# Key-major score pieces of a cross-attention kernel dealt over slots 1 to 7 of a unit by the matmul work of each slot

## What is computed

```
q = x @ Wq.T + bq;  k = ctx @ Wk.T + bk;  v = ctx @ Wv.T + bv        (split into 16 heads of 32)
att = softmax(q k^T / sqrt(32))                                      (per head, 224 x 750)
out = x + (att @ v) @ Wo.T + bo
out = (out - mean) / sqrt(var + 1e-5) * gamma + beta                 (over the 512)
```

## Time and profile before

| | |
|---|---|
| median of 3 runs | 680.19 us (678.84 to 680.62) |
| the profiled execution, its time | 678.81 us |
| the profiled execution, its span | 676.4 us |
| mean granted clock of PE | 0.988 |
| busy PE / DVE / ACT / POOL | 645.8 / 476.1 / 331.9 / 455.4 us |

### The profile page before, as it was taken

How to read it: one execution, slowest core, us unless ns; L and a number is a source line. 1 busy time by engine, 2 the same in 40 slices (tenths; PEclk the granted TensorE clock), 3 DMA queues, 4 the chain that set the end, 5 groups by cost and what they waited for, 6 DMA issues and landing times.

```text
span 676.4 us, 15102 instructions
## 1 busy us (share of the span) xinstructions
PE 645.8 (95%) x5433; PEld 448.0 (66%) x5433; DVE 476.1 (70%) x680; ACT 331.9 (49%) x657; POOL 455.4 (67%) x458
## 2 busy tenths in 40 slices
PE   6999999999999999999999999999999999997893
PEld 5756666766767666776767667776677767664451
DVE  4657667787767786777767787677867877664875
ACT  4514545455555455554455545555455545543470
POOL 9302765866967588576857679575867759675962
PEclk9999999999999999999999999999999999998798
DMA  9383323232232223332233322322233201330010
GB/s 289 113 210 89 82 75 75 53 95 51 74 98 70 65 74 86 85 71 88 56 82 84 88 74 56 95 70 67 83 81 90 51 1 41 93 80 23 1 56 28
DMA packets 39514, 53.08 MB, mean 78 GB/s; under 512 B 13388, under 2 KB 25688, under 8 KB 39448
## 3 DMA queue, kind: packets, MB, share of 16 engines
q1 hardware_dynamic: 39448, 52.16, 28.9%
HBM read 24.52 MB, written 3.67 MB: 42 GB/s over the span
## 4 chain that ended last, share of the span: by engine, by line
PE 86%; DVE 7%; issue 3%; POOL 2%; DMA 1%; ACT 1%; SPq 0%; POOLq 0%; DVEq 0%; ACTq 0%
PE ps_task L472 38%; PE ps_scores L483 11%; PE ps_task L521 11%; PE ps_scoresT L507 10%; PE ps_task L436 6%; PE ps_scores L472 3%; PE ps_task L446 2%; DVE top L741 2%; PE ps_task L547 2%; DMA ctx_in<-in_ctx 1%; DVE y L715 1%; PE ps_scoresT L492 1%; PE ps_task L450 1%; POOL pair_sums L850 1%; DVE parts L703 1%
## 5 line engine op out<-in xcount | busy, mean ns | idle before, releaser
L741 DVE TENSOR_REDUCE top<-ps_scores 112x1 f32<-112x750 f32 x256 | 235.4, 926 | 120.7 <-PE ps_scores L483 120.3
L850 POOL TENSOR_TENSOR pair_sums<-probsT 125x672 f32<-125x672 f32 x122 | 198.8, 1629 | 174.8 <-ACT probsT L642 169.7
L642 ACT ACTIVATE probsT<-ps_scoresT 125x448 f32<-125x448 f32 x384 | 189.0, 548 | 111.2 <-PE ps_scoresT L507 107.8
L483 PE MATMUL ps_scores<-stacks 96*112 96x512 f16 (+1 forms) x512 | 125.6, 327 | 4.3 <-DVE top L741 3.0
L472 PE MATMUL ps_task<-wvT,ctxT 128*125 128x512 f16 x552 | 127.2, 380 | 0.7 <-DVE ctxT L705 0.6
L472 PE MATMUL ps_task<-ctxT,wkT 128*128 128x375 f16 x696 | 120.7, 323 | 0.1
L507 PE MATMUL ps_scoresT<-stacks 100*125 100x224 f16 x768 | 116.9, 265 | 2.3 <-ACT probsT L642 0.4
L507 PEld LDWEIGHTS ps_scoresT<-stacks 100*125 100x125 f16 x768 | 81.6, 136 | 35.2 <-ACT probsT L642 18.4
L472 PEld LDWEIGHTS ps_task<-wvT,ctxT 128*125 128x125 f16 x552 | 73.0, 136 | 38.9 <-DVE ctxT L705 0.9
L472 PEld LDWEIGHTS ps_task<-ctxT,wkT 128*128 128x128 f16 x696 | 67.6, 97 | 36.8 <-DVE v L708 0.5
L855 POOL TENSOR_TENSOR head_sums<-pair_sums 125x224 f32<-125x224 f32 x122 | 84.5, 693 | 10.4
(11 more groups left out here) (96 smaller groups left out, 599.2 us busy)
## 6 DMA issues: line engine op xcount, KB each, us to landing
stacks<-parts SPq DMA_DIRECT2D x256, 60.9 KB, 2.0
ctx_in<-in_ctx SPq DMA_DIRECT2D x16, 672.0 KB
stacks<-parts SPq DMA_DIRECT2D x128, 46.9 KB, 2.0
x_in<-in_x SPq DMA_DIRECT2D x8, 448.0 KB, 3.7
resid<-in_x SPq DMA_DIRECT2D x8, 448.0 KB, 3.8
out_y<-y SPq DMA_DIRECT2D x16, 224.0 KB, 2.3
stacks<-parts SPq DMA_DIRECT2D x128, 14.0 KB, 1.8
ctx_in<-in_ctx SPq DMA_DIRECT2D x16, 78.0 KB
```

Source lines behind the costliest of these rows:

```text
L483: last = nc.tensor.matmul(ps_scores[0:QP, s % RING, keys], stacks[0:STACK_ROWS, g, h, NK + QP * q:NK + QP * q + QP], stacks[0:STACK_ROWS, ...
L642: nc.scalar.activation(probsT[0:KP, g % 2, h, 2 * j:2 * j + 2, :].rearrange("p k q -> p (k q)"), ps_scoresT[0:KP, piece % 2, 0:2 * NQ], AC ...
L741: nc.vector.tensor_reduce(top[0:QP, g % 2, HG * q + h:HG * q + h + 1], ps_scores[0:QP, s % RING, 0:NK], AX.X, ALU.max).then_inc(top_ready, 1)
L850: nc.gpsimd.tensor_tensor(pair_sums[0:KP], probsT[0:KP, g % 2, h, 0:3, :], probsT[0:KP, g % 2, h, 3:6, :], ALU.add).then_inc(pair_sums_rea ...
```

## The change

It replaces the rule for the pieces by a table over the 32 steps, and in the visit's slot it puts the pieces behind the attends and ahead of the sums. In a unit the pieces still come in their order and are still twelve. Slot 0 has none, slot 1 has two; of the steps with transposes, 2, 6, 10, 12, 20 and 23 have one, 14 has two and 16 (a slot 0) none; steps 30 and 31 have one each; the others have two. ACT's iteration follows the same function, so its two first exps of a unit move to slot 1, ahead of the copy.

```diff
+    PIECES_IN = (0, 2, 1, 2, 2, 2, 1, 2,  0, 2, 1, 2, 1, 2, 2, 2,  0, 2, 2, 2, 1, 2, 2, 1,  0, 2, 2, 2, 2, 2, 1, 1)
...
+    assert all(sum(PIECES_IN[i:i + UNIT]) == PIECES for i in range(0, STEPS, UNIT))
...
         def pieces_of(s):
 
-            i = s % UNIT
-            return (2 * i - 4, 2 * i - 3) if i >= 2 else ()
+            of_slot = PIECES_IN[UNIT * (s // UNIT):s + 1]
+            return range(sum(of_slot[:-1]), sum(of_slot))
...
                         if s % UNIT == 0:
                             turn_maxima(u, (g - 1) % UNITS)
-                        for piece in pieces_of(s):
-                            scores_keymajor(u, (g - 1) % UNITS, piece)
+                        if s % UNIT != VISIT:
+                            for piece in pieces_of(s):
+                                scores_keymajor(u, (g - 1) % UNITS, piece)
                     if due(("attend", 0), b, s) and not (isinstance(b, int) and b == B):
                         pe.wait_ge(task_saved, before + saved_by(b, s - TASK_BANKS))
                     for k in range(KT):
                         for u, g_u in due(("attend", k), b, s):
                             attend(u, g_u, k, b if g >= 2 else b - 1, parity if g >= 2 else 1 - parity)
+                    u = unit_before(b, g, 1)
+                    if u is not None and s % UNIT == VISIT:
+                        for piece in pieces_of(s):
+                            scores_keymajor(u, (g - 1) % UNITS, piece)
                     for u, g_u in due("sum_keys", b, s):
                         sum_keys(u, g_u)
```

## The result

The changed kernel takes 685.25 us (median of 4, 685.04 to 686.95) against 679.52 us (median of 4) for the kernel before: a ratio of 1.0083, 95% interval 1.0064 to 1.0102. It is slower, by 0.8%. The forecast was 685.1 us, within 681.7 to 688.3. The profiled execution was the slowest of the four, 686.95 us around a span of 684.8.

A forecast was written before the change was run, and what follows sets the result against it. PE, busy 77.29 of a middle batch's 77.48 us, was taken as the bound. Hand-overs +7.3, stalls -2.2 and batch 7 -0.2 gave +4.9 us on the 680.19 us median: 685.1 us, range 681.7 to 688.3.

The forecast's parts named there:

- The hand-over, 0.28 us a visit: Pieces between attends and sums: one more round trip into 32-column work, 0.28 us a visit, +7.3 us over 26 visits.
- Maxima and copy cost nothing: In the visit, piece 0's wait for ACT's maxima and the later copy of the sums add nothing.
- The stalls, unit by unit: Steps with one piece: unit 0 -0.30, unit 1 -0.15 and -0.11, unit 2 +0.19, unit 3 0 us a batch.
- unit 1: Slot 11's stall goes, -0.15 us; slots 12 and 13 give -0.11, between -0.35 and +0.10; slot 14's stall stays.
- Slot 21 lost what slot 20 gave: Unit 2: the piece removed from slot 20 returns as wait for DVE's save in slot 21, +0.19 us.
- the -0.37: Sum of the stall changes per full batch, -0.37 us; -2.2 us for six batches, batch 0 left at 0.
- Batch 7, -0.2 forecast: Last batch, no next one to prepare: stalls, visit, slot 17 and slot 25 sum to -0.2 us.
- three sub-steps: Batch 7: stalls after slots 2 and 6 -0.65 us, POOL's head sum at slot 17 -0.46, slot 25 +0.66.
- the final slots at 0: Final slots of batch 7: same pieces and as many hand-overs, so 0 us.
- A (free hand-over): Rival: hand-over between last attend and piece 0 is free; -2.9 us in all, 677.3 us; chance 0.07.
- D (the copy holds PE): Rival: the visit's exps delay the copy, holding PE in slots 2 and 3; +5.2 us, 690.3 us; chance 0.04.
- B (all stalls go): Rival: dealing clears every short stall, slot 21's DVE wait too; 1.3 us a batch, 679.4 us; chance 0.08.
- C (the clock is kept in slot 18 of batch 7): Rival: slot 17's wait ends sooner, PE may keep 2.4 GHz; -1.7 us, 683.4 us; chance 0.11.

The follow-up runs named there:

- the hand-over alone: Kernel before the change, no piece moved; in the visit's slot the next step's two score matmuls stand between attends and sums: 694.95 us, ratio 1.022.
- the fastest kernel: Changed kernel with the visit's pieces ahead of the attends and the old deal (two pieces in slots 2 to 7) in units 2 and 3: 675.26 us, ratio 0.9935.

## Why the prediction was right

**The hand-over, 0.28 us a visit.** Right in size and in parts (0.12, 0.13, 0.03 forecast; 0.11, 0.14, 0.03 measured), and shown as the cause of the loss in a middle batch by four runs: absent with the pieces behind the sums or ahead of the attends, present with no piece moved, and the same for one piece as for two. Reading it from the tail of the old kernel, where the very order already stood, was what made it exact.

**Maxima and copy cost nothing.** Right for batches 5 and 6: PE has no such wait in slots 1 to 3, and with the same ACT order but the pieces ahead of the attends the loss goes. In batches 1 to 4 of the changed kernel there is a small wait that the prediction put at nothing: the first pair behind the visit in units 2 and 3 takes 0.46 to 0.68 us to the next task for 0.39, about 1 us in all. In slot 18 of batch 1 PE's weight load (PEld) waits for ACT's exps. They start 0.88 us behind the visit's pair there, and 0.45 in batch 6; why is open:

```profile
152.12 0.60 PE L509 MATMUL ps_scoresT<-stacks 100*125 100x224 f16 x4
153.00 0.98 ACT L649 ACTIVATE probsT<-ps_scoresT 125x448 f32<-125x448 f32 x2 [2.41 <-PE ps_scoresT L509]
153.60 0.19 PEld L509 LDWEIGHTS ps_scoresT<-stacks 100*125 100x125 f16 x2 [0.25 <-ACT probsT L649]
```

**The stalls, unit by unit.** Forecast for a middle batch, hand-over included: unit 2 +0.47, unit 3 +0.28, unit 0 -0.02, unit 1 +0.02, in all +0.75. Measured from attends to attends: +0.46, +0.28, -0.01, -0.07, in all +0.66. The doubtful one was unit 1: the stall of slot 13 left whole (0.19 us), where I had allowed 0.11 for slots 12 and 13, and slot 15 stayed at 0.58 us, so DVE followed PE a little further than I allowed. Slot 21 lost what slot 20 gave, as said, and the run with slot 20 refilled gives the 0.20 us back.

**Batches 0 to 6 together** lost 3.7 us by slot 17 of batch 6, where the same terms count 24 x 0.28 - 6 x 0.56 (units 0 and 1) + 5 x 0.19 (unit 2) = 4.3. The term at fault is the -0.37, which I took from the late batches; the loss per batch was below 0.75 us in five of the six intervals from slot 17 to slot 17 (0.39, 0.54, 0.58, 0.57, 0.84, 0.66). In batches 1 to 4 the parts differ from the late ones and partly cancel. Unit 0 won 0.16 to 0.17 us and unit 1 0.20 to 0.48, as the pairs of slots 3 and 11 had taken 0.68 us there and not 0.53; unit 2 lost 0.55 to 0.83 and unit 3 0.37 to 0.40, with the wait for the exps above.

**Batch 7, -0.2 forecast.** Here three sub-steps were off. Slots 3 and 7 kept 0.33 us of stall each instead of 0.2 and 0.3. POOL's second head did start 0.44 us earlier behind the value task, but the sums came no earlier: one of POOL's adds took 1.08 us instead of 0.69. It lay over a scaling of DVE's, which in the kernel before had begun 0.26 us ahead of the add (the last section has such a pair; here it is not tested):

```profile
614.30 1.08 POOL L862 TENSOR_TENSOR head_sums<-pair_sums 125x224 f32<-125x224 f32 x1
614.48 0.38 DVE L762 TENSOR_TENSOR attn<-attn_sums,recip 128x224 f32<-128x224 f32 x1
```

And from slot 25 to the last turn of the maxima the changed kernel lost 0.48 us, not 0.66. The scores of slot 26 came 0.96 us later, as a pair, a round trip and more time in the attends (4.64 us for 4.34) stood ahead of them, but DVE was not the bound all the way: its scaling took 0.38 us for 0.67, and the old turn had come 0.24 us behind the maxima, released by an exp. PE's wait in slot 17, in the answer on PE's waits:

```profile
PE ps_task L549 <- POOL head_sums L865: 3.0, 1, 3.0
```

It shrank from 3.52 to 3.01 only because a pair of pieces now stands in it. At the last turn of the maxima the changed kernel was 4.9 us late (652.94 against 648.03): the forecast's sum, with a shortfall of 0.6 in the middle and an excess of 0.7 from slot 17 of batch 6 on that cancelled, which is luck.

**The last 3.5 us of the profiled execution** are the step that failed: the prediction has the final slots at 0, as they hold the same pieces and as many hand-overs. From the last turn to the end the changed kernel took 31.8 us, the one before 28.4. The windows over the same kind of work, of the changed kernel and of the one before:

```profile
655.90:662.00 6.10, 6.10 (x49) 2.71 (x48) 2.59 (x2) 2.50 (x5) 3.14 (x3) 0.50 0.01 3
```

```profile
649.90:655.80 5.90, 5.87 (x87) 3.16 (x86) 3.31 (x4) 4.41 (x9) 4.28 (x5) 1.00 0.06 17
```

Here PE ran at half its clock, 1.2 GHz, and made 49 matmul records in 6.10 us where 87 took 5.90. Just ahead stood its waits for DVE's maxima (1.33 us) and for an exp (0.44). In the kernel before the turn had waited 0.76 us. The windows of 14 us from the last turn, of the changed kernel, the one before, the hand-over alone and the fastest kernel, in this order:

```profile
652.94:666.94 14.00, 13.46 (x146) 6.77 (x146) 7.50 (x6) 7.48 (x16) 5.80 (x6) 0.76 0.10 32
648.03:662.03 14.00, 13.90 (x186) 7.67 (x187) 8.51 (x9) 8.52 (x17) 6.01 (x6) 1.00 0.11 35
664.66:678.66 14.00, 13.91 (x187) 7.67 (x188) 8.57 (x9) 8.50 (x17) 5.48 (x5) 1.00 0.11 35
641.87:655.87 14.00, 12.98 (x166) 6.73 (x170) 7.36 (x7) 8.08 (x16) 5.98 (x6) 0.88 0.11 35
```

The granted clock of this window is 0.76 or 0.88 in all nine profiled executions with a table of pieces, which take 30.9 to 32.2 us from the last turn to the end, and 1.00 in the two without (28.4 us each). So in the profiles the lower clock comes with the table, which also deals the pieces of the final slots anew. There is one profile of each kernel, and no run tests which of the waits ahead brings it. It doesn't stand in the medians in full: the other three executions of the changed kernel have spans of 682.5 to 683.5 us.

**The total.** The sum to the last turn was right, the end was not, and the median came out at 685.25 against 685.1 with some luck. The forecast put its 4.9 us on a median of 680.19 us, while the profiled execution, whose rows it used, was 1.4 us faster. Between the two profiled executions the change costs 8.1 us (686.95 against 678.81), between the medians of four 5.7.

**The rivals.** A (free hand-over) and D (the copy holds PE) are ruled out for the middle batch by the rows of the visit. B (all stalls go) fails at slot 21, and also at slot 15, where the pair still takes 0.58 us and the value task still starts 0.06 us behind DVE's save. C (the clock is kept in slot 18 of batch 7) did not happen: the output projection took 4.44 us there, 4.09 before.

## What to carry to other kernels

On an engine that is busy for more than 99% of a batch, read distances between starts, not waits: this loss had no wait to its name. Keep all matmuls of one column-tiled kind together, and put filler work ahead of or behind the whole group, where something else covers its consumer. Before thinning a slot, see which engine ends the wait behind it: the stalls at slots 3, 7 and 11 were ACT's and went, while slot 21's was DVE's and took back what slot 20 gave.

## What was not expected of the hardware

DVE's multiplication of two SBUF operands (128 x 224, 0.38 us) stood still until POOL's sum of SBUF operands ended: 1.40 us beside a POOL instruction of 1.61, 0.98 us beside two halves of 1.91 together. Both times the scaling ended 0.25 us behind POOL's instruction. The reciprocals, with one SBUF operand, kept their 0.84 us beside POOL. The Trainium skill states this on the page "SBUF — State Buffer", under "Who interferes with whom": a DVE instruction with two SBUF inputs contends with a GpSimd instruction that reads SBUF, and the one that comes second is blocked until the first ends. By that rule, the trace agrees, with these numbers. In batch 7 of the changed kernel it was POOL's add that grew (1.08 us), though by the profile DVE's scaling of 0.38 us started 0.18 us behind it; which of the two came second there the rough starts on POOL don't tell. The block explains most of what one piece in slot 10 instead of slot 14 cost: the scaling was 1.02 us longer than in the fastest kernel, of 1.33 us in the batch.
